# Tables of a per-item pipeline on Trainium2: W1 in long rows ahead of W2, gamma behind the first x, b2 and beta spread over the partitions by TensorE

## The reference

```python
# 1: attention pooling, one of three masks by prompt type (0, 1, 2)
s = tanh(x @ W1a + b1a) @ v
p = softmax(where(mask[type], s, -1e30))
x = x + (p @ x) / count(mask row)
# 2: adapter of language lang (10 of them), then layer norm
h = relu(x @ W1[lang] + b1[lang])
u = x + h @ W2[lang] + b2[lang]
x = x + (u - mean(u)) * rsqrt(var(u) + 1e-5) * gamma[lang] + beta[lang]
# 3: reaction and diffusion with the item's zX, zY, zR
x = x + zX * lap_columns(x) + zY * lap_rows(x) + zR * x * (1 - x)
# 4: category matrix of cat (64 of them)
x = x + x @ W3[cat] + b3[cat]
```

## Time and profile before

| | us |
|---|---|
| runs | 1118.82, 1113.79, 1120.64; median 1118.82 |
| profiled execution, its own time | 1114.18 |
| its span, first to last instruction | 1112.4 |
| PE busy in the span | 1051.4 (95%) |
| DVE busy | 961.6 (86%) |
| POOL busy | 710.2 (64%) |
| ACT busy | 495.7 (45%) |
| bytes moved | 273.95 MB, mean 246 GB/s |

### The profile page before, as it was taken

How to read it: one execution, slowest core, us unless ns; L and a number is a source line. 1 busy time by engine, 2 the same in 40 slices (tenths; PEclk the granted TensorE clock), 3 DMA queues, 4 the chain that set the end, 5 groups by cost and what they waited for, 6 DMA issues and landing times.

```text
span 1112.4 us, 23554 instructions
## 1 busy us (share of the span) xinstructions
PE 1051.4 (95%) x4892; PEld 658.1 (59%) x4892; DVE 961.6 (86%) x1965; ACT 495.7 (45%) x1410; POOL 710.2 (64%) x652
## 2 busy tenths in 40 slices
PE   2489999999999999999999999999999999999996
PEld 1356665665666556666666656665666565565652
DVE  3288998998899889999899999988998898998984
ACT  0244444444444444444454444444444444444441
POOL 0066667657667676667667666666766766766765
PEclk9999999999999999999999999999999999999999
DMA  9478888788888988877787778898888788888873
GB/s 382 179 219 260 272 244 257 235 235 236 281 247 237 308 257 265 233 212 228 237 249 223 224 233 266 254 276 242 253 246 259 234 264 249 273 267 219 251 232 113
DMA packets 136182, 273.95 MB, mean 246 GB/s; under 512 B 29288, under 2 KB 29296, under 8 KB 128496
## 3 DMA queue, kind: packets, MB, share of 16 engines
q1 hardware_dynamic: 97600, 202.45, 60.2%
q10 hardware_dynamic: 38448, 70.01, 20.8%
HBM read 248.26 MB, written 33.55 MB: 253 GB/s over the span
## 4 chain that ended last, share of the span: by engine, by line
issue 32%; POOL 31%; PE 24%; DVE 9%; DMA 2%; DVEq 1%; POOLq 0%; ACT 0%; ACTq 0%; SPq 0%
POOL b_wide L817 12%; PE ps_out L390 10%; POOL neighbours L798 7%; POOL react L804 6%; POOL rstd L790 4%; DVE x L709 4%; PE bank_hidden L344 3%; PE ps_attn L322 3%; PE ps_adapt L372 3%; PE ps_pool L363 2%; DVE res L684 2%; DMA xts<-in_xT 2%; POOL above L810 2%; PE ps_x3T L380 1%; PE bank_scores L333 1%
## 5 line engine op out<-in xcount | busy, mean ns | idle before, releaser
L390 PE MATMUL ps_out<-w3s,x3T 128*128 x1024 | 489.5, 601 | 2.3 <-ACT x3T L441 2.3
L810 POOL TENSOR_TENSOR above<-above,below 128x512 f32<-128x512 f32 x128 | 164.6, 1286 | 255.8 <-DMA above<-x 255.3
L390 PEld LDWEIGHTS ps_out<-w3s,x3T 128*128 128x128 f32 x1024 | 185.2, 191 | 189.7 <-issue 188.1
L709 DVE SCALAR_TENSOR_TENSOR x<-above,zy_t,react 128x512 f32<-128x512 f32 x128 | 209.4, 1636 | 10.5 <-POOL above L810 8.9
L804 POOL TENSOR_TENSOR react<-react,x 128x512 f32<-128x512 f32 x128 | 179.8, 1405 | 2.1 <-ACT react L484 2.1
L817 POOL TENSOR_TENSOR b_wide<-b_wide,x 128x512 f32<-128x512 f32 x128 | 178.0, 1391 | 1.8 <-DMA b_wide<-in_b 1.8
L344 PE MATMUL bank_hidden<-w_all,xts 128*128 x1024 | 137.7, 278 | 23.6 <-DMA xts<-in_xT 23.6
L344 PEld LDWEIGHTS bank_hidden<-w_all,xts 128*128 128x128 f32 x1024 | 125.1, 193 | 54.1 <-issue 52.4
L790 POOL TENSOR_TENSOR rstd<-var_eps,minus_half 128x1 f32<-128x1 f32 x128 | 69.9, 546 | 133.1 <-DVE var_eps L676 133.1
L462 ACT ACTIVATE square_junk<-ps_adapt,neg_mean 128x512 f32<-128x512 f32 x128 | 88.0, 688 | 133.7 <-DVE neg_mean L639 133.7
L372 PE MATMUL ps_adapt<-w_all,hid 128*128 x256 | 133.6, 604 | 12.5 <-DVE x L691 12.1
(11 more groups left out here) (97 smaller groups left out, 1252.1 us busy)
## 6 DMA issues: line engine op xcount, KB each, us to landing
w3s<-in_w SPq DMA_DIRECT2D x128, 1024.0 KB
xts<-in_xT ACTq DMA_DIRECT2D x128, 256.0 KB, 4.9
xs<-in_x ACTq DMA_DIRECT2D x128, 256.0 KB, 5.4
b_wide<-in_b SPq DMA_DIRECT2D x128, 256.0 KB, 4.7
out_x<-res SPq DMA_DIRECT2D x128, 256.0 KB, 3.3
below<-x SPq DMA_DIRECT2D x128, 252.0 KB
above<-x SPq DMA_DIRECT2D x128, 252.0 KB
below<-x SPq DMA_DIRECT2D x256, 2.0 KB
```

The source lines that it names most:

```text
L390: mm = pe.matmul(ps_out[j.ring(2)][:, :], x3T[:, j.ring(2), k * P:(k + 1) * P], w3s[:, bass.ds(wslot * (K * D) + k * D, D)], start=(k == 0 ...
L709: nc.vector.scalar_tensor_tensor(x3[:, q, :], above[:, q, :], zy_t[:, bass.ds(i.n, 1)], react[:, q, :], ALU.mult, ALU.add).then_inc(x3_rea ...
L810: nc.gpsimd.tensor_tensor(above[:, q, :], above[:, q, :], below[:, q, :], ALU.add).then_inc(rows_ready, 1)
```

## The change

The DMAs of b2, beta and b1 are gone, and W1 and gamma are moved:

- W1 is laid out on the host as 128 rows of 20 KB, like W2, and SP issues it ahead of W2. ACT no longer does.
- SP waits for item 0's transposed x (`xT_in[0]`) before it issues gamma.
- b1 comes with the columns of small values, which are now 15 rows instead of 5, and `relu` takes its bias from `vals`.
- b2 and beta come as `lrows`, 32 rows of 512 (10 of b2, 10 of beta, 12 of zeros) three times over, 96 partitions in all. ACT rounds them to bf16 in `lang_parts`; POOL takes the difference in the first 64 partitions; ACT rounds that; POOL takes the next difference in the first 32. So the three blocks of partitions hold three bf16 parts whose sum is the float32 row.
- PE spreads a row in one bf16 matmul: the stationary operand is column `row` of `pick16` (ones at the three partitions of that row), repeated 128 times, and the moving one is `lang_parts` (96 x 512). The row stands then in all partitions of a PSUM bank. ACT moves the ten rows of b2 to SBUF, DVE those of beta, each from two banks in turn. Two b2 spreads are ahead of the sort, two behind it, and the rest, with those of beta, behind the four products of line 311.
- DVE's 16 table operations become one copy of the bank (`wide_rows`), and nine operations on POOL, with `item_tables` counting the two results. `attn_scores` waits for `score_tables`, which DVE raises with `ident16`.
- For item 0 alone, PE does `attn_project` ahead of `adapter_project`, and ACT `attn_tanh` ahead of `move_xw`; `attn_project` waits for x itself. ACT's moves of b2 4 to 9 are in slot 0, behind the issue of x for items 0 and 1.

```diff
             sp.dma_start(ids_i[:, :], ids).then_inc(ids_in, 16)
             sp.dma_start(col_rows[:, :], cols).then_inc(ids_in, 16)
+            sp.dma_start(w1_all[:, :], w1l).then_inc(w1_in, 16)
             sp.dma_start(w2_all[:, :], w2l).then_inc(w2_in, 16)
-            for wide_table, rows, loaded in ((b2_wide, b2l, b2_in), (beta_wide, beta, beta_in),
-                                             (gamma_wide, gamma, gamma_in)):
-                sp.dma_start(wide_table[:, :], rows.rearrange("l d -> (l d)").partition_broadcast(P)
-                             ).then_inc(loaded, 16)
+            sp.wait_ge(xT_in[0], 16)
+            sp.dma_start(gamma_wide[:, :], gamma.rearrange("l d -> (l d)").partition_broadcast(P)
+                         ).then_inc(gamma_in, 16)
...
+            def spread_row(bank, row, done):
+                pe.matmul(bank[:, :], pick16[:, row:row + 1].broadcast_to([3 * ROWS, P]), lang_parts[:, :],
+                          start=True, stop=True).then_inc(done, 1)
+
+            def spread_b2(i):
+                if i >= 2:
+                    pe.wait_ge(b2_moved, i - 1)
+                spread_row(b2_banks[i % 2], i, b2_spread)
+
+            def spread_beta(i):
+                if i >= 2:
+                    pe.wait_ge(beta_moved, i - 1)
+                spread_row(beta_banks[i % 2], L + i, beta_spread)
+
+            pe.wait_ge(pick_made, 1)
+            pe.wait_ge(row_rest, 2)
+            spread_b2(0)
+            spread_b2(1)
+
             def sort_param(what):
                 to = ps_params[:, what * B:(what + 1) * B] if what < LANG else \
                     ps_params_end[:, (what - LANG) * B:(what - LANG + 1) * B]
                 sort_param(what)
             pe.wait_ge(place_made, 2)
             sort_param(WSLOT).then_inc(sorted_made, 1)
+            spread_b2(2)
+            spread_b2(3)
             pe.wait_ge(wide_made, 1)
             for i in range(4):
                 mm = pe.matmul(ps_wide[:, i * P:(i + 1) * P], wide[:, i * P:(i + 1) * P], place[:, :],
                                start=True, stop=True)
             mm.then_inc(sorted_made, 1)
...
+            for i in range(L):
+                if i >= 4:
+                    spread_b2(i)
+                spread_beta(i)
 
             def attn_project(a):
                 r = a.ring(2)
+                pe.wait_ge(xT_in[r], a.dma())
...
+                if (s + 1).is_first:
+                    attn_project(s + 1)
+                    adapter_project(s + 1, lang_p1)
+                elif (s + 1).inside(B):
                     adapter_project(s + 1, lang_p1)
                     attn_project(s + 1)
...
-            act.dma_start(w1_all.rearrange("p (l n) -> p l n", l=L), w1l.rearrange("l p n -> p l n")).then_inc(w1_in, 16)
-            act.dma_start(b1_all[:, :], b1l).then_inc(b1_in, 16)
+            act.dma_start(lang_rows[:, :], lrows).then_inc(lrows_in, 16)
...
+            act.wait_ge(lrows_in, 16)
+            nc.scalar.activation(lang_parts[:, :], lang_rows[:, :], ACT.Copy).then_inc(row_parts, 1)
+            act.wait_ge(row_rest, 1)
+            nc.scalar.activation(lang_parts[0:2 * ROWS, :], lang_rows[0:2 * ROWS, :], ACT.Copy
+                                 ).then_inc(row_parts, 1)
+
+            def move_b2(i):
+                act.wait_ge(b2_spread, i + 1)
+                nc.scalar.activation(b2_wide[:, i * D:(i + 1) * D], b2_banks[i % 2][:, :], ACT.Copy
+                                     ).then_inc(b2_moved, 1)
+
+            for i in range(4):
+                move_b2(i)
...
-                nc.scalar.activation(hid[:, f.ring(2), :], ps_hid, ACT.Relu, bias=b1_all[:, bass.ds(lang, 1)]
+                nc.scalar.activation(hid[:, f.ring(2), :], ps_hid, ACT.Relu, bias=vals[:, bass.ds(lang + B1L, 1)]
...
+                if h.is_first:
+                    act.wait_ge(item_tables, 2)
...
+                if s.is_first:
+                    for i in range(4, L):
+                        move_b2(i)
...
+                if s.is_first:
+                    attn_tanh(s)
+                    move_xw(s)
+                elif s.inside(B):
                     move_xw(s)
                     attn_tanh(s)
...
+            dve.wait_ge(consts_made, 1)
+            then(nc.vector.tensor_tensor(pick[:, :], ident[0:3 * ROWS, 0:ROWS], ident[0:3 * ROWS, ROWS:2 * ROWS],
+                                         ALU.add))
+            nc.vector.tensor_tensor(pick16[:, :], pick[:, :], ident[0:3 * ROWS, 2 * ROWS:3 * ROWS], ALU.add
+                                    ).then_inc(pick_made, 1)
             dve.wait_ge(ids_in, 16 * 2)
             nc.vector.tensor_copy(ids_rows[:, :], ids_i[:, :])
-            dve.wait_ge(consts_made, 1)
             nc.vector.tensor_copy(vals[:, ITEM:ITEM + 1], iota_col[:, :]).then_inc(ids_cast, 1)
 
...
+            nc.vector.tensor_copy(ident16[:, :], ident[:, :]).then_inc(score_tables, 1)
...
+            nc.vector.tensor_copy(wide_rows[:, :], ps_wide[:, :]).then_inc(tables_made, 1)
+            for i in range(L):
+                dve.wait_ge(beta_spread, i + 1)
+                nc.vector.tensor_copy(beta_wide[:, i * D:(i + 1) * D], beta_banks[i % 2][:, :]
+                                      ).then_inc(beta_moved, 1)
...
+                if b.is_first:
+                    dve.wait_ge(item_tables, 1)
...
+                    dve.wait_ge(b2_moved, L)
...
+                    dve.wait_ge(beta_moved, L)
...
+            pool.wait_ge(row_parts, 1)
+            nc.gpsimd.tensor_tensor(lang_rows[0:2 * ROWS, :], lang_rows[0:2 * ROWS, :], lang_parts[0:2 * ROWS, :],
+                                    ALU.subtract).then_inc(row_rest, 1)
+            then(nc.gpsimd.tensor_scalar(from_top[:, :], iota_col[:, :], 1.0, None, ALU.add))
+            then(nc.gpsimd.tensor_scalar(from_end[:, :], iota_col[:, :], -1.0, float(S), ALU.mult, ALU.add))
+
+            pool.wait_ge(row_parts, 2)
+            nc.gpsimd.tensor_tensor(lang_parts[0:ROWS, :], lang_rows[0:ROWS, :], lang_parts[0:ROWS, :],
+                                    ALU.subtract).then_inc(row_rest, 1)
+
             pool.wait_ge(tables_made, 1)
+            first_kind, second_kind, third_kind = (kind_parts[:, i * B:(i + 1) * B] for i in range(3))
+            nc.gpsimd.tensor_scalar(first_kind, kind_t, 0.0, from_top[:, 0:1], ALU.is_equal, ALU.mult)
+            nc.gpsimd.tensor_scalar(third_kind, kind_t, 1.5, float(S - 1), ALU.is_gt, ALU.mult)
+            then(nc.gpsimd.tensor_scalar(second_kind, kind_t, 1.0, from_end[:, 0:1], ALU.is_equal, ALU.mult))
+            then(nc.gpsimd.tensor_tensor(count_t[:, :], first_kind, second_kind, ALU.add))
+            nc.gpsimd.tensor_tensor(count_t[:, :], count_t[:, :], third_kind, ALU.add).then_inc(item_tables, 1)
+            then(nc.gpsimd.tensor_tensor(c0_t[:, :], zx_t, zy_t, ALU.add))
+            nc.gpsimd.tensor_scalar(nzr_t[:, :], zr_t, -1.0, None, ALU.mult)
+            then(nc.gpsimd.tensor_scalar(c0_t[:, :], c0_t[:, :], -2.0, 1.0, ALU.mult, ALU.add))
+            nc.gpsimd.tensor_tensor(c0_t[:, :], c0_t[:, :], zr_t, ALU.add).then_inc(item_tables, 1)
 
             def inverse_std(h):
                 q = h.ring(2)
         "x": x,
         "xT": tiles(x.transpose(0, 2, 1)),
         "ids": np.stack([np.asarray(i) for i in (itok_B_0_63, itok_B_0_8, itok_B_0_2)]),
-        "cols": np.stack([np.asarray(c) for c in (condB_zX, condB_zY, condB_zR, L0_cond_v, L0_cond_b1)]),
+        "cols": np.stack([np.asarray(c) for c in (condB_zX, condB_zY, condB_zR, L0_cond_v, L0_cond_b1)]
+                         + list(np.asarray(L1_cond_b1))),
```

More of the change, by code:

```diff
@@ L17 @@
 CAT, FRESH, WSLOT, ITEM, LANG, KIND, NPARAM = 0, 1, 2, 3, 4, 5, 6
-ZX, ZY, ZR, V, B1A, NVAL = 6, 7, 8, 9, 10, 11
-NID, NCOL = 3, 5
+ZX, ZY, ZR, V, B1A, B1L = 6, 7, 8, 9, 10, 11
+NID = 3
+ROWS = 32
 class Step:
@@ L64, in cond_residual_kernel @@
 def cond_residual_kernel(nc, x, xT, ids, cols, w1a,
-                         w1l, b1l, w2l, b2l, gamma, beta, w3, b3, out):
+                         w1l, w2l, lrows, gamma, w3, b3, out):
     B, S, D = x.shape
@@ L70, in cond_residual_kernel @@
     C = w3.shape[0]
+    NCOL = cols.shape[0]
+    NVAL = ZX + NCOL
     ctx = ExitStack()
@@ L91, in cond_residual_kernel @@
         w2_all = sb("w2_all", [P, L * D])
-        b1_all = sb("b1_all", [P, L])
         b2_wide = sb("b2_wide", [P, L * D])
@@ L98, in cond_residual_kernel @@
         masks16 = sb("masks16", [P, 3 * P], BF16)
-        tables_mark = sb("tables_mark", [P, 1])
+        from_top = sb("from_top", [P, 1])
+        from_end = sb("from_end", [P, 1])
         iota_row = sb("iota_row", [P, P])
@@ L104, in cond_residual_kernel @@
         count_t = sb("count_t", [P, B])
-        zx_t = sb("zx_t", [P, B])
-        zy_t = sb("zy_t", [P, B])
+        wide_rows = sb("wide_rows", [P, 4 * B])
+        zx_t, zy_t, zr_t, kind_t = (wide_rows[:, i * B:(i + 1) * B] for i in range(4))
+        kind_parts = sb("kind_parts", [P, 3 * B])
         nzr_t = sb("nzr_t", [P, B])
```

(38 more changed lines are left out.)

22 lines of the change are left out of this document (removed).

## The result

The changed kernel takes 1092.01 us (median of 6 runs, 1089.82 to 1097.21) where the kernel before took 1119.22; the ratio is 0.9767, with a 95% interval of 0.9737 to 0.9798. A second set (experiment 6) gave 0.9764 (0.9737 to 0.9792). Over all runs, the means are 1092.2 (12 runs) and 1118.1 (77 runs of before, those timed beside the experiments): 25.9 us less. I had forecast 17.0 less.

What follows compares the result with a forecast made beforehand. PE paces the items, and the head waits for the first x's DMA. An earlier start of 15.4 us plus 1.6 in the first item makes 17.0 off 1116.9: 1099.9, forecast 1100.0 us, range 1094 to 1107.5.

Steps and rivals of the forecast that it cites:

- a body that is 98 to 99% PE passes a shift on in full: Loop over the 128 items: the whole earlier start, summed at 17.0 us, reaches the total time.
- The level: Baseline for the whole kernel: mean of four runs, 1116.9 us, from which 17.0 was subtracted.
- The DMA part: Head loads: W1 lands at 10, W2 16 to 17, x 17.6 to 19, gamma near 26 with 9 us cover.
- The work that replaces it: Head split and spreads of b2 and beta: split done about 8.7, first projection at 21.8 instead of 37.16, 15.4 gained.
- in step: Head: ACT's b2 moves 4 to 9 end by 21.6 at the latest, alongside DVE's beta copies at 21.5 to 22.1.
- The first item: First projection to transposed mix of item 0: faster clock 2.4 us or swapped order 0.4; taken as 1.6.
- The sum: Earlier start 15.4 plus first item 1.6 gives 17.0 us gained.
- The low clock: Head spreads: PE stays at or falls back to 1.2 GHz; gain 14.2, time 1102.7 us; chance 0.20.
- The late split: Head: language rows stuck behind W1's packets, up to 4.2 us later; gain 12.8, time 1104.1; chance 0.10.
- x did land right behind W2: Head: x still waits behind W2's tail, start 23.2 instead of 21.8; time 1101.3 us; chance 0.05.
- The slower body: Items' loop: DVE's mix left behind POOL operations loses more than the head gains; to 1113, chance 0.06; to 1130, 0.04.
- The Trainium skill's rule that I quoted: Head: exclusive DVE/POOL port lock could make DVE's ranking wait about 1.5 us instead of 0.3; sum 15.8.

Runs made afterwards that it cites:

- experiment 6: The changed kernel unmodified, run again: median 1091.38 us, ratio 0.9764; also the changed kernel without the swapped order at item 0, no time given.
- the second profile: The changed kernel unmodified, run and profiled once more: median 1091.38 us.
- Experiment 1: The changed kernel with 27 idle copies on ACT ahead of the issue of the first x: mean 1115.0 us, ratio 0.997.
- before aligned: The kernel before with 192 B of padding per partition ahead of x2, so six tensors start at multiples of 256 B: mean 1112.9 us, ratio 0.9943.
- 2: The kernel before with W1 in 20 KB rows ahead of W2 on SP, and b2, beta, gamma DMAs behind the first x: mean 1105.4 us.
- 4: The changed kernel with gamma issued right behind W2, without waiting for the first x: mean 1099.7 us.
- 7: The kernel before with W1 in 20 KB rows, still in ACT's queue: mean 1111.6 us.
- the second kernel of experiment 3: The changed kernel without spreads of rows 5 to 9 of b2 and beta, zeros written by DVE behind the first mix: mean 1097.3 us.
- experiment 3: The changed kernel without spreads of rows 5 to 9 of b2 and beta; zeros by POOL in the head, mean 1095.9 us, or by DVE later, 1097.3.

## Why the prediction was wrong

- **"... a body that is 98 to 99% PE passes a shift on in full."** This is the step that failed. The body passed the shift on, but the sum had no term for the body itself: I took it that a change of the preparation can't reach the items. Through SBUF addresses it did, for some 5 us (3.1 to 7.4 by the comparison taken), and by PE's clock in the first slots for an estimated 1 to 3. None of my rivals looked at the allocation, though the diff shows the new tensors and their sizes.
- **The level.** I built on 1116.9, a mean of four; over 77 runs it is 1118.1. The profile that I took the body from was one without a low clock in the first slots. That hid a part of the gain from me, by my estimate 1 to 3 us: I priced the clock for item 0 and not for items 1 to 3.
- **The DMA part** held: W1 at 10.5 (10 forecast), W2 at 16.6 (16 to 17), x issued at 14.14 (15.0), landed at 17.2 (17.6 to 19). In the second profile all of it is later: W1 at 13.0, W2 at 19.2, x at 19.6. Gamma landed at 28.7, not 26, and was wanted at 31.56, not 35: cover 2.8 us instead of 9.
- **The work that replaces it** was 1.3 us quicker than I had it. The split was done at 8.43 (8.7), spreads cost the chain 0.43 and 0.22 us each, as taken, and the ranking waited for POOL 0.24 us once. But I let the wide products and the four spreads run at the low clock until 15.6, and PE was at the high one from about 12, so DVE's copies began at 13.9 and not near 15.7. They didn't set the start either: ACT did, which I had "in step". Start 20.5, and 22.2 in the second profile; forecast 21.8.
- **The first item** gained 2.65 us (6.65 to 4.0), where I took 1.6 as a mean over the two levels of the clock.
- **The sum.** From the first mixes (43.2 and 24.95, means of the profiles) the head gave 18.2, against 17.0 forecast. The first slots add an estimated 1 to 3 by the clock, alignment some 5. Together that is 24 to 26, measured 25.9. Experiment 1 splits it otherwise: it has the aligned rows and the first mix of before, so alignment is the 3.1 us that it kept, and 4.6 behind the first mix came back with the early start. The intervals of the two (0.6 to 6 for the 3.1, 3.8 to 9 for the ratio of before aligned) overlap; how the 7.7 us outside the head divide between clock and alignment stays open.
- **The rivals.** The low clock did not come in the changed kernel (its first eight products took 1.13 us), but experiments 1, 2, 4, 6 and 7 had it, and the kernel before in some runs. The late split did not occur. x did land right behind W2 in both profiles, but ahead of the last spread, so it wasn't the bound; it was in the second kernel of experiment 3. The slower body was the wrong sign. The Trainium skill's rule that I quoted ("SBUF — State Buffer", the shared port pair) is borne out in experiment 3, and more fully than I allowed: a tensor_scalar waited not for the rest of one POOL instruction but for that and the next, 3.26 us for an operation of 0.28. In the changed kernel itself it cost the 0.24.

## What to carry to other kernels

Where two DMA queues share the engines packet by packet, put long rows in the queue whose data is wanted first, and keep small pieces out of the way of the transfer that starts the pipeline. After a long stand of PE, count the low clock for the first slots too; 100 idle products ahead of the first item made only that item quicker. And before a gain in a long loop is put down to a change ahead of it, compare the addresses of the tensors that DMAs read and write in the loop; padding to 256 B costs nothing to try.

## What the runs showed of the hardware

- Tensors in SBUF that DMAs read and write in 2 KB rows: 64 B off a multiple of 256 cost 5.2 us in one kernel, and 7.4 with some low clock in it in the other, over 128 items; 4.9 by the traces from item 8 on. Which tensor counts was not separated.
- A table's size is not what holds back the other queue; its packets' size is. W1 landed at 36.3 us in pieces of 2 KB and at 14.9 in rows of 20 KB, in the same place of the same queue. Gamma issued beside x made x land 9.0 us after its issue instead of 3.1, and 128 rows of 40 B took some 6 us beside 20 KB rows.
- A long stand of PE costs twice: at once (2.07 us instead of 1.08 for eight products), and again for some slots after it, in some runs and not in others (26.8 to 29.9 us for four slots of one and the same kernel). The low clock also came without such a stand, in the changed kernel with unaligned rows (30.3).
- Two of POOL's memsets of 2560 columns (2.22 us each), one behind the other, both held up a DVE tensor_scalar with one tensor input that began before the second (3.26 us instead of 0.28).
